# A state-space scan whose two half-products and two half-scans of each step become one instruction each

## The reference

```
x_dbl = hidden @ W_xproj.T                    # low-rank step size (64), B (16), C (16)
delta = softplus(dt_low @ W_dt.T + b_dt)      # (b, l, d)
dA    = exp(delta[..., None] * A)             # (b, l, d, n),  A = -exp(A_log), n = 16
dBx   = (delta * x)[..., None] * B[:, :, None, :]
h     = dA_t * h + dBx_t                      # over the 128 positions l, h = 0 at the start
y     = sum over n of h * C_t
```

## Time and profile before

| | |
|---|---|
| median of 3 runs | 1446.86 us (1442.95 to 1447.52) |
| the profiled execution | 1447.94 us |
| its span, first to last instruction | 1446.1 us |
| scan steps on DVE | 27.4 to 507.0 us of the span |
| mean granted TensorE clock | 0.913 |

### The profile page before, as it was taken

The page is one execution under the profiler, slowest core; times in us unless marked ns, Lnnn a source line. Parts: engine busy times, 40 slices in busy tenths (PEclk is TensorE's granted clock), DMA queues, the critical chain, the costliest instruction groups (busy, mean ns, idle before and its releaser), DMA issues. The chain is left out here.

```text
span 1446.1 us, 25901 instructions
## 1 busy us (share of the span) xinstructions
PE 1104.2 (76%) x8527; PEld 762.4 (53%) x8527; DVE 1019.3 (70%) x1875; ACT 748.1 (52%) x1605; POOL 805.4 (56%) x720
## 2 busy tenths in 40 slices
PE   5877778777787758888888886122999999999940
PEld 1322323222232237666676664022899899999940
DVE  2999999999999946677767765784455555555423
ACT  4666566575666436555666563100555555555425
POOL 2677676767768636666766764335144554455230
PEclk8999999999999979999999998555999999999975
DMA  3000000000000010111111100103134443343235
GB/s 103 15 15 1 15 0 15 15 0 15 0 0 0 1 28 27 35 33 33 33 41 36 33 32 26 65 1 101 56 63 107 94 106 81 89 112 55 24 47 215
DMA packets 42311, 64.00 MB, mean 44 GB/s; under 512 B 8161, under 2 KB 34465, under 8 KB 39073
## 3 DMA queue, kind: packets, MB, share of 16 engines
q1 hardware_dynamic: 29376, 41.92, 8.9%
q0 software_dynamic: 12288, 17.05, 7.2%
q10 hardware_dynamic: 576, 4.19, 0.7%
HBM read 42.00 MB, written 21.14 MB: 44 GB/s over the span
## 5 line engine op out<-in xcount | busy, mean ns | idle before, releaser
L514 POOL TENSOR_TENSOR scan_hc<-scan_state,scan_c_sb 128x1024 f32<-128x1024 f32 x128 | 304.1, 2380 | 142.9 <-DVE scan_state L442 132.0
L442 DVE TENSOR_TENSOR_SCAN scan_state<-scan_decay,scan_drive_ps 128x512 f32<-128x512 f32 x256 | 297.4, 1203 | 0.2
L223 PE MATMUL scan_y_ps<-scan_hc,all_ident 128*128 128x512 f32 x520 | 254.7, 613 | 2.1 <-POOL scan_hc L514 2.1
L1660 DVE TENSOR_TENSOR expert_hid_lo<-expert_hid,expert_hid_hi 128x512 fp32r<-128x512 f32 x128 | 88.5, 692 | 177.4 <-ACT expert_hid_hi L1644 165.7
L1557 POOL DMA_INDIRECT acc<-expert_rows,expert_lst x64 | 112.8, 1763 | 180.4 <-DVE expert_rows L1686 165.2
L1639 ACT ACTIVATE expert_hid<-expert_h_ps,expert_b 128x512 f32<-128x512 f32 x128 | 88.0, 688 | 200.0 <-PE expert_h_ps L556 191.9
L326 ACT ACTIVATE scan_decay<-scan_delta,scan_a_neg 128x508 f32<-128x508 f32 x256 | 169.2, 715 | 7.4 <-POOL scan_delta L496 7.2
L435 DVE TENSOR_TENSOR scan_drive_ps<-scan_dx,scan_b_ps 128x512 f32<-128x512 f32 x256 | 162.3, 679 | 14.6 <-POOL scan_dx L501 10.7
L368 ACT ACTIVATE scan_c_sb<-scan_c_ps 128x512 f32<-128x512 f32 x128 | 76.5, 598 | 138.2 <-PE scan_c_ps L216 129.2
L556 PE MATMUL expert_o_ps<-weights_w_hi,expert_hid_lo 128*128 128x256 f32 x512 | 143.4, 280 | 0.0
L554 PE MATMUL expert_o_ps<-weights_w_hi,expert_hid_hi 128*128 128x256 f32 x512 | 143.4, 280 | 0.0
(11 more groups left out here) (226 smaller groups left out, 2543.5 us busy)
## 6 DMA issues: line engine op xcount, KB each, us to landing
weights_w<-w SPq DMA_DIRECT2D x16, 1024.0 KB
table<-all_row SPq DMA_DIRECT2D x32, 132.0 KB, 1.8
scan_xT<-xT SPq DMA_DIRECT2D x8, 512.0 KB, 3.9
attn_ctxT<-ctxT SPq DMA_DIRECT2D x32, 128.0 KB, 2.4
acc<-all_row SPq DMA_DIRECT2D x32, 128.0 KB, 1.7
final_a<-acc SPq DMA_DIRECT2D x4, 1024.0 KB, 7.2
out<-final_o ACTq DMA_DIRECT2D x4, 1024.0 KB, 5.8
expert_b<-b SPq DMA_DIRECT2D x8, 128.0 KB
```

Of the source, the lines that this page charges most:

```text
L223: last = pe.matmul(y_ps[k][:], ident[0][:], hc[:, n % RING, k, :], start=False, stop=(n == NS - 1))
L442: dve.tensor_tensor_scan(state[:, n % RING, k, :], decay[:, n % RING, k, :, :].rearrange("p b t -> p (b t)"), drive_ps[k][:], 0.0, ALU.mul ...
L514: pool.tensor_tensor(hc[:, n % RING, :, :], state[:, n % RING, :, :], c_sb[:, n % RING, :].unsqueeze(1).broadcast_to([P, KH, GT]), ALU.mul ...
L1660: dve.tensor_tensor(hid_lo[:, f % RING_H, :], hid[:, f % 2, :], hid_hi[:, f % RING_H, :].bitcast(F32), ALU.subtract).then_inc(hid_ready, 1)
```

## The change

`drive_ps` becomes one tile of 2 x 512 columns. A step has one product of 1024 columns, in which `b_ps` is read twice through a broadcast axis, and one scan of 1024 columns over both halves. The semaphores `drive_ready` and `scanned` count steps instead of halves. The scan waits for both decays.

```diff
-        drive_ps = [s.ps(f"drive{i}", [P, 512]) for i in range(KH)]
+        drive_ps = s.ps("drive", [P, KH, 512])
...
-                    pe.wait_ge(drive_ready, KH * q + 1)
+                    pe.wait_ge(drive_ready, q + 1)
...
-                    act.wait_ge(scanned, KH * (q + 1))
+                    act.wait_ge(scanned, q + 1)
...
-                    for k in range(KH):
-                        dve.wait_ge(scanned, KH * (q + RING - 1) + k + 1)
-                        dve.tensor_tensor(drive_ps[k][:], dx[par][:, k, :], b_ps[:], ALU.mult).then_inc(drive_ready, 1)
+                    dve.wait_ge(scanned, q + RING)
+                    dve.tensor_tensor(drive_ps[:], dx[par][:], b_ps[:].unsqueeze(1).broadcast_to([P, KH, 512]), ALU.mult).then_inc(drive_ready, 1)
...
                     dve.wait_ge(hc_ready, q + 1)
-                    for k in range(KH):
-                        dve.wait_ge(drive_ready, KH * q + k + 2)
-                        dve.wait_ge(decay_ready, KH * (q + 1) + k + 1)
-                        dve.tensor_tensor_scan(state[:, n % RING, k, :],
-                                               decay[:, n % RING, k, :, :].rearrange("p b t -> p (b t)"),
-                                               drive_ps[k][:], 0.0, ALU.mult, ALU.add).then_inc(scanned, 1)
+                    dve.wait_ge(drive_ready, q + 2)
+                    dve.wait_ge(decay_ready, KH * (q + 2))
+                    dve.tensor_tensor_scan(state[:, n % RING, :, :].rearrange("p k t -> p (k t)"),
+                                           decay[:, n % RING, :, :, :].rearrange("p k b t -> p (k b t)"),
+                                           drive_ps[:].rearrange("p k t -> p (k t)"), 0.0, ALU.mult, ALU.add).then_inc(scanned, 1)
...
-                dve.sem_inc(scanned, KH * RING)
+                dve.sem_inc(scanned, RING)
...
-                    pool.wait_ge(scanned, KH * (q + 1 + RING))
+                    pool.wait_ge(scanned, q + 1 + RING)
```

## The result

| | before | after |
|---|---|---|
| median | 1446.04 us (4 runs) | 1478.1 us (4 runs, 1476.75 to 1479.01) |
| ratio | | 1.0224, 95% interval 1.0204 to 1.0243 |
| span of the profiled execution | 1446.1 us | 1477.2 us |
| scan steps on DVE, first product to L1119 (after: L1117) | 27.4 to 507.0 us | 27.4 to 536.7 us |

The change makes the kernel 2.2% slower, 32 us. The forecast was 12 us, with 1470 as the upper end of the range: the sign was right and the size was not. Of the 31.1 us by which the span grew, 29.7 lie in the scan steps.

A forecast was written before the change was run, and what follows sets the result against it. DVE bounds the scan phase. Joined product and scan with 0.035 us after each make a step 3.552 us against 3.416; over seven groups and the last, 10.3 + 2.1 = +12.4 us on 1446.86, about 1459 us, range 1451 to 1470.

The forecast's parts named there:

- DVE sets the end, and a us of its step is a us of the phase: Scan phase: DVE works 461.4 of 478.5 us and bounds it; the phases behind only shift with it.
- What joining saves: Per step on DVE: one product of 1.213 us and one scan of 2.269 us, together 3.482 us.
- Scan to product costs 0.035 us: Boundary from scan's end to next product: overlap of about 0.08 us lost, start 0.035 us after the end.
- Product to scan costs 0.035 us: Boundary from product's end to its scan: overlap lost, scan starts 0.035 us after the end.
- the 0.19 of the earlier trace: Gap ahead of L455 before the change, not used because a DVE queue semaphore increment lies between wait and instruction.
- rows 8: Earlier trace: L1672 waits for L1670 in front of it and starts 0.03 us after its end.
- rows 9: Earlier trace: L1040 waits for L1037, starts 0.03 us after its end, taken to have a second, long fulfilled wait.
- L418's wait as a cushion: Steps 7 and 8 of 7 groups: slowdown vanishes in 1.62 us of waiting; total wait 11.4 to about 10.
- waiting costs nothing, fewer instructions win: Rival at both product-scan boundaries: overlaps kept, step 0.114 us less, -13.4 us, 1433.5 us; chance 5 in 100.
- more is lost: Rival: boundaries cost up to 0.19 us (1491), or two-tile PSUM instructions pay the start again (1492); chance 8 in 100.

The follow-up runs named there:

- the waits in the best order: Changed kernel with the scan's waits for ring slot and decays moved ahead of the product, leaving only the product wait between; 1465.07 us, ratio 1.0133.
- the run with the wait last: Changed kernel with the scan's waits for product and decays swapped, so the product wait comes last; 1472.01 us, ratio 1.0197.

## Why the prediction was right in sign and wrong in size

- *DVE sets the end, and a us of its step is a us of the phase*: right. 29.7 us more on DVE's steps, 31.1 more in the span.
- *What joining saves*: nearly right. Product and scan together measure 1.229 + 2.286 = 3.515 us against 3.482 forecast. Over 128 steps the 0.033 us more are 4 us. For the product the reason is in the trace: it lasts 1.229 us when it starts from standing and 1.204 where it follows L453 and overlaps it. For the scan there is no such pair of rows here; its 2.269 was twice the product's cost by column, and that is 0.017 low.
- *Scan to product costs 0.035 us*: right in the loop, 0.03. In the last two groups it is 0.10, about 2 us in all.
- *Product to scan costs 0.035 us*: this is the step that failed. It is 0.19 to 0.20 us in 84 of the 128 steps, 0.48 in one and 0.08 to 0.13 in the rest. The idle time ahead of L440 is 21.2 us where the forecast had 128 x 0.035 = 4.5, so 16.7 us more. The 4 and the 2 us above come on top. Against them stand 2.5 us that L418's wait gave back beyond the forecast (7.5 us left instead of 10), and two single waits of the kernel before, behind the last step of the loop's first and second pass, which its DVE waits show and those of the changed kernel don't:

```profile
DVE scan_drive_ps L435 <- issue: 1.1, 1, 1.1
DVE scan_drive_ps L435 <- DVE scan_state L442: 1.0, 1, 1.0
```

The forecast had left these two as they were. Together this is 16.7 + 4 + 2 - 2.5 - 2.1 = 18.1 us; the excess to explain in the steps is 29.7 - 12.4 = 17.3. The 0.8 us between them were not traced.
- The reason for that miss lies in how I chose the rows. The argument ran "a wait for the neighbour costs 0.03" from the earlier trace rows, and it set aside the 0.19 of the earlier trace rows, because a semaphore increment stands there behind the wait. That was the right sort of difference to look for and the wrong conclusion. What counts is whether *anything* in the queue has still to be done once the awaited signal comes, and in the changed scan it does: a bare wait and a register computation. In rows 8 the wait is alone on the instruction. It is so in rows 9 too, and there the prediction misread them: it took L1040 to carry "a second, long fulfilled wait as the scan has", but in the trace that second wait is a queue instruction of its own (L576, 21 ns), done before L1037 starts, and L1040 carries only the wait for L1037. The order of the three waits in the diff hinted at the queue's, and I read them as a set.
- *L418's wait as a cushion*: right as a mechanism, but it falls from 11.4 to 7.5 us and not to 10, since the steps in front of it grew by more than forecast.
- The rival "waiting costs nothing, fewer instructions win" falls: the run with the new waits alone is 38 us slower than the kernel before. The rival "more is lost" had the right size in its first form (a boundary of up to 0.19 us), and had been given 8 in 100; it was right for one of the two boundaries, and its time of 1491 us, which charged both, was too high. Its second form, that an instruction over two PSUM tiles pays its start again, is not seen: the scan is 2.286 us long, and the whole change is 5 us faster than its waits alone.

## What to carry to other kernels

Two instructions of half the size on one engine cover each other's completion; joined, each must see its neighbour finished. Here those waits alone cost 38 us, and the change with its joined instructions gave some 5 of it back, 18 with the waits in the best order; no joined version reached the kernel before. Before joining, ask who waits for whom directly in the queue, and whether other work can stand between.

Where an instruction must wait for its direct neighbour, nothing else should stand between the two: foreign waits and register computations belong ahead of the first of them. The same dependence cost 0.04, 0.10 or 0.20 us here by that alone. Look for this in the trace's queue records, since the order there need not be that of the source: here the wait for the product came in the queue ahead of the one for `hc_ready`.

Which memory an operand lies in can matter more than the order: moving one scan operand from PSUM to SBUF cost 94 us against the changed kernel, because POOL was working from SBUF at the same time.

## What the runs showed of the hardware that I had not expected

- What stands in DVE's queue behind a released wait sets the gap. From the product's end to the scan's start it is 0.03 to 0.04 us when the scan carries that wait itself, 0.10 with one bare wait between (0.09 when that bare wait, for two semaphores, had been standing there while the product ran, and 0.13 in the last two groups of the run with the wait last), 0.12 to 0.13 with one register instruction between, and 0.19 to 0.20 with a bare wait and a register instruction. In every one of these places, and in rows 9, the tensor instruction itself carries one wait in the trace; a further one is a queue instruction ahead of it. So do the changed kernel's products in the last two groups: they carry the wait for B, the one for the scan stands bare in front of them, and their gap is 0.10 instead of 0.03.
- A DVE scan that reads two operands from SBUF and a POOL product that reads SBUF exclude each other, and the waiting appears in the record as duration (3.33 us for a scan of 2.29), not as idle time. A view of waits alone would have called DVE busy. It holds the other way round: the L512 recorded from 306.48 lasts 2.86 us instead of 2.35, and started while L423, with two inputs in SBUF, was running.
- A DVE product that starts from standing is recorded 0.025 us longer than one that starts in the overlap of its predecessor (1.229 against 1.204).
